# Two staging slots, a second DMA queue and ScalarE in the weight quantiser; preparation of the next tile placed ahead of the conv work in stage A

## The chip, the cores and the metric

The kernel runs as one program on the 8 cores of one Trainium2 chip. Each core computes one half of one batch entry's output; there are no messages between the cores. The metric is the device time in microseconds (us) of the slowest core. Engines of a core: TensorE (PE) for matmuls, VectorE (DVE), ScalarE (ACT), GpSimd (POOL), and SyncE (SP), which here only issues DMAs. POOL issues DMAs too; they stand on a queue of their own.

## The reference

One "macaron" layer: half an FFN, an attention-like recurrent block, and half the same FFN again. The layout is channels on partitions, positions along the free axis.

```
x = x + 0.5 * ffn(layernorm(x))
x = x + ssm_and_recurrence(layernorm(x))
x = x + 0.5 * ffn(layernorm(x))

ffn:  h = bit_linear(x, w1)            # 1024 -> 4096
      h = silu(depthwise_conv1d(h))    # 3 taps along the sequence
      return bit_linear(h, w2)         # 4096 -> 1024
bit_linear: act_quant:   s = 127 / max|x| per position; clip(round(x*s), -128, 127)/s
            weight_quant: s = 1 / mean|w|;              clip(round(w*s), -1, 1)/s
```

The rounding is done by adding a large constant and subtracting it again (columns `cmag` and `cnmag`).

## The kernel before

The program is written by hand, engine by engine, with counting semaphores. What is written down first for an engine runs first on it: an engine takes its own instructions in program order and waits where a wait is written. The helper `Sem.wait(engine)` without a value waits for everything that has been counted on that semaphore up to this point of the text, so a wait's place in the text also decides how much it waits for. Semaphores: `sv` DVE, `sa` ACT, `sp` PE, `sev` PSUM evictions, `sy` DMAs of SP, `sg` DMAs of POOL.

The stages in order of time:

- **Quantise w1** (`quant_weights`, 8 chunks of 128x4096 f32, 2 MB each). First loop: a chunk is loaded into the one staging slot (L350) and DVE sums its absolute values (L352). A few tiny operations turn the sums into the scale. Second loop: each chunk is loaded again (L381), DVE does three passes over it (L383 scale and add the magic constant, L386 subtract it and clip above, L390 clip below into `wq` as bf16), and SP stores the chunk to HBM (L392) for the second FFN. With one slot a load starts when DVE is done with the chunk before.
- **Stage A of FFN 1** (`ffn_stage_a`, 17 tiles of 256 positions with 2 of halo). A tile has 8 groups (`q` = 0 to 7). A group is 4 output banks of 8 matmuls each (L457, 32 in all), then ACT starts the conv from the banks (L466), DVE adds the two other taps (L474, L482; L482 also frees the banks), and ACT does Silu (L493). The matmuls of the next group wait for L482, as there are 4 banks. After Silu the text issues one step of the preparation of the next tile's input: `c_load` (group 0), `c_stats` (1), `c_ln` (2), `c_quant` (3), `c_smul` (4), `c_xq` (5). These use DVE, PE and ACT. After group 7 comes the quantisation of the tile's 4096 hidden channels (L297 to L529), which the change does not touch.
- **Quantise w2** (same function, 32 chunks of 128x1024 f32, 512 KB each), then **stage B of FFN 1** (matmuls with w2).
- **The middle block** (layer norms, scan, 18 sweeps of the recurrence, output projection), about 4500 to 7030 us.
- **Stage A of FFN 2** (9 tiles, the same function) and **stage B of FFN 2**. The quantised weights come back from HBM on POOL's queue.

Stage A therefore has 26 tiles, of which 24 prepare a next one (16 and 8).

Of the kernel before, what the change touches and what calls it, by code (L numbers as in the profile page):

```python
# [10 lines left out]
AF = mybir.ActivationFunctionType  # L11
ALU = mybir.AluOpType
AX = mybir.AxisListType
ds = bass.ds

P = 128
# [54 lines left out]
def build_nc(debug=False):  # L71
# [41 lines left out]
    with st:  # L113
        def sb(name, shape, dt=F32, stk=None):
            _nm[0] += 1
            return (stk or st).enter_context(nc.sbuf_tensor(f"{name}_{_nm[0]}", shape, dt))
# [8 lines left out]
        cmag = sb("cmag", [P, 1])  # L125
        cnmag = sb("cnmag", [P, 1])
# [4 lines left out]
        swcol = sb("swcol", [P, 1])  # L131
# [16 lines left out]
        cm = sb("cm", [P, 512])  # L148
# [17 lines left out]
        sy = Sem(st, nc, "sy")  # L166
        sg = Sem(st, nc, "sg")
        sv = Sem(st, nc, "sv")
        sa = Sem(st, nc, "sa")
# [4 lines left out]
        V, SC, T, G, SY = nc.vector, nc.scalar, nc.tensor, nc.gpsimd, nc.sync  # L174

        def tnop_inc(sem):
            T.drain()
            sem.inc(T.nop())

        def dma_fence():  # L180
            SY.wait_ge(sy.h, sy.n) if sy.n else None  # L181
            G.wait_ge(sg.h, sg.n) if sg.n else None

        def bar():
            dma_fence()
            nc.all_engine_barrier()
# [157 lines left out]

        def quant_weights(wsrc, nchunks, width, wq_t, wqhbm, rw_dst, wscb,
                          rw_scale=1.0 / 127.0):
            for c in range(nchunks):
                sv.wait(SY)
                dma_fence()
                sy.inc(SY.dma_start(wscb[:, 0:width], wsrc[c * P:(c + 1) * P, :]), 16)  # L350
                sy.wait(V)
                sv.inc(V.tensor_reduce(cm[:, c:c + 1], wscb[:, 0:width], AX.X,  # L352
                                       ALU.add, apply_absolute_value=True))
            V.drain()
            V.tensor_reduce(hmt[:, 0:1], cm[:, 0:nchunks], AX.X, ALU.add)
            sv.inc(V.drain())
            sv.wait(T)
            T.matmul(pst[0:1, 0:1], hmt[:, 0:1], onesf[:, 0:1], start=True, stop=True)
            tnop_inc(sp)
            sp.wait(V)  # L360
            V.tensor_scalar(r11[0:1, 0:1], pst[0:1, 0:1], 1.0 / (nchunks * P * width),
                            None, ALU.mult)
            V.drain()
            V.tensor_scalar(r11[0:1, 0:1], r11[0:1, 0:1], 1e-5, None, ALU.max)
            V.drain()
            V.reciprocal(r11[0:1, 1:2], r11[0:1, 0:1])
            V.drain()
            V.tensor_scalar(r11[0:1, 2:3], r11[0:1, 0:1], rw_scale, None, ALU.mult)
            sv.inc(V.drain())
            sv.wait(T)  # L370
            T.matmul(pst[0:P, 8:9], onesr[0:1, 0:P], r11[0:1, 1:2], start=True, stop=True)
            T.matmul(pst[0:P, 9:10], onesr[0:1, 0:P], r11[0:1, 2:3],
                     start=True, stop=True)
            tnop_inc(sp)
            sp.wait(V)
            V.tensor_copy(swcol[:, 0:1], pst[0:P, 8:9])
            V.tensor_copy(rw_dst[:, 0:1], pst[0:P, 9:10])
            sv.inc(V.drain())
            for c in range(nchunks):
                sv.wait(SY)  # L380
                sy.inc(SY.dma_start(wscb[:, 0:width], wsrc[c * P:(c + 1) * P, :]), 16)  # L381
                sy.wait(V)
                V.tensor_scalar(wscb[:, 0:width], wscb[:, 0:width], swcol[:, 0:1],  # L383
                                cmag[:, 0:1], ALU.mult, ALU.add)
                V.drain()
                V.tensor_scalar(wscb[:, 0:width], wscb[:, 0:width], cnmag[:, 0:1], 1.0,  # L386
                                ALU.add, ALU.min)
                V.drain()
                dst = wq_t[:, c * width:(c + 1) * width]
                sv.inc(V.tensor_scalar(dst, wscb[:, 0:width], -1.0, None, ALU.max))  # L390
                sv.wait(SY)
                sy.inc(SY.dma_start(wqhbm[c * P:(c + 1) * P, :], dst), 16)  # L392
            bar()

        def ffn_stage_a(wq, abuf, src_hbm, c0list, yq_hbm):
# [50 lines left out]
            for ti in range(nt):  # L446
                c0 = c0list[ti]
                xq_t = xqs[ti % 2]
                nxt = (prep_chunks(ti + 1, c0list[ti + 1]) if ti + 1 < nt
                       else [])  # L450
                sv.wait(T)
                for q in range(HC // 4):
                    for j in range(4):
                        mh = 4 * q + j
                        sev.wait(T, sev.n - 3 + j)
                        for kd in range(DC):
                            mm = T.matmul(pb[j][:, 0:tw],  # L457
                                          wq[:, kd * HD + mh * P:kd * HD + (mh + 1) * P],
                                          xq_t[:, kd * tw:(kd + 1) * tw],
                                          start=(kd == 0), stop=(kd == DC - 1))  # L460
                        sp.inc(mm)
                    sp.wait(SC)
                    SC.drain()
                    for j in range(4):
                        mh = 4 * q + j
                        a1 = SC.activation(tg[:, (mh % 8) * TOA:(mh % 8 + 1) * TOA],  # L466
                                           pb[j][:, 0:tw - 2], AF.Identity,
                                           bias=convbs[:, mh:mh + 1],
                                           scale=convws[:, 3 * mh:3 * mh + 1])
                    sa.inc(a1)  # L470
                    sa.wait(V)
                    for j in range(4):
                        mh = 4 * q + j
                        V.scalar_tensor_tensor(tg[:, (mh % 8) * TOA:(mh % 8 + 1) * TOA],  # L474
                                               pb[j][:, 1:tw - 1],
                                               convws[:, 3 * mh + 1:3 * mh + 2],
                                               tg[:, (mh % 8) * TOA:(mh % 8 + 1) * TOA],
                                               ALU.mult, ALU.add)
                    V.drain()
                    for j in range(4):  # L480
                        mh = 4 * q + j
                        ev = V.scalar_tensor_tensor(tg[:, (mh % 8) * TOA:(mh % 8 + 1) * TOA],  # L482
                                                    pb[j][:, 2:tw],
                                                    convws[:, 3 * mh + 2:3 * mh + 3],
                                                    tg[:, (mh % 8) * TOA:(mh % 8 + 1) * TOA],
                                                    ALU.mult, ALU.add)
                        sev.inc(ev)
                    sv.inc(V.engine_nop())  # L488
                    sv.wait(SC)
                    SC.drain()  # L490
                    for j in range(4):
                        mh = 4 * q + j
                        a2 = SC.activation(y2[:, mh * TOA:(mh + 1) * TOA],  # L493
                                           tg[:, (mh % 8) * TOA:(mh % 8 + 1) * TOA],
                                           AF.Silu)
                    sa.inc(a2)
                    if nxt:
                        nxt.pop(0)()
                sa.wait(V)
                quant_cols(y2, HC, TOA, None, 2,  # L500
                           acol_dst=a2col[:, c0 // 128:c0 // 128 + 2], halves=2)
# [83 lines left out]
        with ffn1:  # L585
# [16 lines left out]
            with sta:  # L602
                abuf = make_stage_a_bufs(sta)
                quant_weights(w1T, DC, HD, wq, wq1buf, rw1c, abuf[5], rw_scale=1.0)
                sv.wait(V)
                V.tensor_scalar(convws[:], convws[:], rw1c[:, 0:1], None, ALU.mult)
                sv.inc(V.drain())
                bar()
                ffn_stage_a(wq, abuf, xT, FF1_A, yqbuf)
            stb = ExitStack()  # L610
            with stb:
                xt = sb("xt", [P, DC * 512], F32, stb)
                yy = sb("yy", [P, DC * 512], F32, stb)
                yqb = sb("yqb", [P, HC * 512], BF16, stb)
                quant_weights(w2T, HC, D, wq, wq2buf, rw2h, yy, rw_scale=1.0)
                sv.wait(V)
                V.tensor_scalar(rw2h[:], rw2h[:], 0.5, None, ALU.mult)
                sv.inc(V.drain())
                bar()
                ffn_stage_b(wq, xt, yy, yqb, xT, FF1_B, yqbuf, x1buf)  # L620
# [455 lines left out]
```

How the kernel before makes its waits and increments, by code:

```python
    def inc(self, instr, by=1):  # L57
        instr.then_inc(self.h, by)
        self.n += by
        return instr
# [1 line left out]
    def wait(self, eng, val=None):  # L62
        v = self.n if val is None else val
        if v > 0:
            eng.wait_ge(self.h, v)
# [5 lines left out]
def build_nc(debug=False):  # L71
# [108 lines left out]
        def dma_fence():  # L180
            SY.wait_ge(sy.h, sy.n) if sy.n else None
            G.wait_ge(sg.h, sg.n) if sg.n else None
# [639 lines left out]
                        hw_marks = [sv.n]  # L822
                        ac_marks = []
                        g_all = 0
                        pend = []
                        for k in range(NSWEEP):
                            parR = (k % 2) * CPAR
                            parW = ((k + 1) % 2) * CPAR
                            for ti, (wi0, tn) in enumerate(UW_T):
                                for kap in range(KC):
                                    trip = ptrip[g_all % 2]
                                    T.wait_ge(sv.h, hw_marks[k])
                                    if g_all >= 2:
                                        sa.wait(T, ac_marks[g_all - 2])
                                    for gi, mpart in enumerate((kap, 4 + kap, 8 + kap)):
```

## Time and profile before

| what | value |
|---|---|
| median of 3 runs | 9121.12 us (9119.67 to 9121.30) |
| profiled execution, its own time | 9118.18 us |
| its span (core 3, the slowest) | 9116.6 us |
| spans of the 8 cores | 9068.4 to 9116.6 us |
| busy: PE, DVE, ACT, POOL | 3693.0, 3885.0, 1955.1, 32.4 us |
| mean granted TensorE clock, all cores | 0.687 to 0.691 |

No engine is busy for half of the span: 43% for DVE, 41% for PE. The time is in chains of waits, stage by stage, and a stage is read from its own rows. The granted clock is a share of full speed: 1.00 is 2.4 GHz, 0.50 is 1.2 GHz. A row of the windows view reads, from left to right: start and end in us, length, busy time (and number of instructions) of PE, of PE's weight loads, of DVE, ACT and POOL, then the granted clock, the mean busy share of the core's 16 DMA engines, and GB/s.

### The profile page before, as it was taken

What the parts mean: (1) busy time and instruction counts of PE and PEld (TensorE: products, weight loads), DVE (VectorE), ACT (ScalarE), POOL (GpSimd) and SP (SyncE); (2) the same over time, 40 slices, a digit from 0 to 9 for tenths busy, and PEclk for the clock granted to TensorE, in tenths of its full rate; (3) what the DMA queues carried; (4) which work ended last, traced back from release to release, by engine and by line L of the source; (5) the groups of instructions that cost most, each with busy time, mean ns of one, the idle gap of its engine ahead of it and who ended that gap; (6) DMA issues with size and microseconds to landing.
All of it is one profiled execution on the core that took longest, in us unless ns stands there. A gap on an engine that the chain in (4) does not pass through costs nothing. (4 is left out here: it accounts for less than half of the span.)

```text
span 9116.6 us, 55112 instructions; the slowest of 8 cores (9068.4 to 9116.6 us)
## 1 busy us (share of the span) xinstructions
PE 3693.0 (41%) x17682; PEld 1957.9 (21%) x17682; DVE 3885.0 (43%) x7213; ACT 1955.1 (21%) x3466; POOL 32.4 (0%) x59
## 2 busy tenths in 40 slices
PE   0222332332332310467522258888852233233257
PEld 0121221221221200223200023433320122122123
DVE  2454555545455432100165534444444454554400
ACT  0122222222222210000000005555530222222200
POOL 0000000000000000000000000000000000000000
PEclk9865665665666655778755579999975566566578
DMA  6200000000000013232211110000024000000042
GB/s 150 83 14 23 19 14 19 23 14 19 23 14 14 23 54 106 99 111 74 93 46 55 37 59 5 1 1 1 1 89 150 19 19 14 19 24 14 23 134 83
DMA packets 311196, 406.89 MB, mean 45 GB/s; under 512 B 20482, under 2 KB 224514, under 8 KB 305154
## 3 DMA queue, kind: packets, MB, share of 16 engines
q1 hardware_dynamic: 305186, 383.44, 13.1%
q0 software_dynamic: 5728, 19.93, 0.7%
q8 instruction: 148, 2.42, 0.1%
q14 instruction: 134, 1.10, 0.0%
HBM read 271.23 MB, written 135.26 MB: 45 GB/s over the span
## 5 line engine op out<-in xcount | busy, mean ns | idle before, releaser
L556 PE MATMUL pb<-yqb,wq 128*128 128x512 bf16 x3584 | 826.7, 396 | 344.1 <-DMA yqb<-yqbuf 222.9
L457 PE MATMUL pb<-xq,wq 128*128 128x258 bf16 x3584 | 623.7, 355 | 568.7 <-DVEq L526 375.0
L474 DVE SCALAR_TENSOR_TENSOR tg<-pb,convws,tg 128x256 f32<-128x256 f32 x832 | 345.1, 477 | 1167.5 <-ACT tg L466 1162.8
L457 PE MATMUL pb<-xqb,wq 128*128 128x258 bf16 x3072 | 531.5, 354 | 499.1 <-DVEq L526 375.3
L841 PE MATMUL pb<-cfc,WhS 128*128 128x512 bf16 (+1 forms) x2880 | 679.8, 365 | 0.0
L466 ACT ACTIVATE tg<-pb,convbs,convws 128x256 f32<-128x256 f32 x832 | 402.8, 566 | 964.7 <-PE pb L457 960.7
L457 PEld LDWEIGHTS pb<-xq,wq 128*128 128x128 bf16 x3584 | 446.5, 127 | 759.0 <-issue 610.7
L332 PE MATMUL pbc<-idsf,repb 128*128 128x128 f32 x316 | 89.4, 408 | 1136.1 <-DVE repb L327 1136.1
L562 DVE SCALAR_TENSOR_TENSOR yy<-pb,rw2h,xt 128x512 f32<-128x512 f32 x112 | 84.1, 751 | 1086.1 <-PE pb L556 1086.1
L556 PEld LDWEIGHTS pb<-yqb,wq 128*128 128x128 bf16 x3584 | 361.7, 101 | 805.9 <-issue 458.5
L457 PEld LDWEIGHTS pb<-xqb,wq 128*128 128x128 bf16 x3072 | 381.1, 126 | 662.4 <-issue 536.8
L522 DVE TENSOR_TENSOR yqa<-y,pbc 128x256 bf16<-128x256 f32 x832 | 280.0, 413 | 546.6 <-ACT y L517 546.6
L493 ACT ACTIVATE y<-tg 128x256 f32<-128x256 f32 x832 | 278.0, 405 | 666.8 <-DVEq L488 666.5
L250 PE MATMUL pst<-xbb,onesb 128*1 128x258 bf16 (+1 forms) x336 | 105.8, 496 | 719.0 <-DVE sqbb L247 719.0
L297 DVE TENSOR_REDUCE cm<-y 128x256 f32<-128x8192 f32 x26 | 359.6, 13832 | 43.3 <-ACT y L493 43.3
L302 PE MATMUL pst<-idsf,cm 128*128 128x128 f32 (+1 forms) x130 | 39.9, 432 | 805.6 <-DVE cm L297 805.6
L482 DVE SCALAR_TENSOR_TENSOR tg<-pb,convws,tg 128x256 f32<-128x256 f32 x832 | 345.0, 477 | 16.5 <-issue 0.9
L836 PE MATMUL pb<-Usb,idsb 128*128 128x512 bf16 (+1 forms) x720 | 262.8, 365 | 199.0 <-ACT tzb L855 111.7
L841 PEld LDWEIGHTS pb<-cfc,WhS 128*128 128x128 bf16 x2880 | 278.0, 103 | 282.6 <-issue 41.1
L841 PE MATMUL pst<-cfc,WhS 128*128 128x512 bf16 (+1 forms) x1440 | 329.1, 356 | 0.0
L515 ACT ACTIVATE y<-y,cmag 128x4096 f32<-128x4096 f32 x52 | 192.9, 3709 | 630.1 <-DVE repb L327 342.4
L861 DVE TENSOR_TENSOR dtb<-tfb,tzb 128x512 f32<-128x512 f32 (+1 forms) x180 | 110.2, 612 | 484.1 <-ACT tzb L855 484.1
(169 smaller groups left out, 4749.1 us busy)
## 6 DMA issues: line engine op xcount, KB each, us to landing
yqb<-yqbuf SPq DMA_DIRECT2D x9, 4096.0 KB
yqbuf<-yqa SPq DMA_DIRECT2D x34, 1024.0 KB
y<-w1T SPq DMA_DIRECT2D x16, 2048.0 KB
yy<-w2T SPq DMA_DIRECT2D x64, 512.0 KB
yqb<-yq2buf SPq DMA_DIRECT2D x5, 4096.0 KB
xt<-xT SPq DMA_DIRECT2D x9, 2048.0 KB
x1buf<-yy SPq DMA_DIRECT2D x9, 2048.0 KB
yq2buf<-yqa SPq DMA_DIRECT2D x18, 1024.0 KB
```

The source lines that it names most:

```text
L297: sv.inc(V.tensor_reduce(cm[:, 0:tw], ap3, AX.X, ALU.max, apply_absolute_value=True))
L457: mm = T.matmul(pb[j][:, 0:tw], wq[:, kd * HD + mh * P:kd * HD + (mh + 1) * P], xq_t[:, kd * tw:(kd + 1) * tw], start=(kd == 0), stop=(kd ...
L466: a1 = SC.activation(tg[:, (mh % 8) * TOA:(mh % 8 + 1) * TOA], pb[j][:, 0:tw - 2], AF.Identity, bias=convbs[:, mh:mh + 1], scale=convws[:, ...
L474: V.scalar_tensor_tensor(tg[:, (mh % 8) * TOA:(mh % 8 + 1) * TOA], pb[j][:, 1:tw - 1], convws[:, 3 * mh + 1:3 * mh + 2], tg[:, (mh % 8) * ...
L482: ev = V.scalar_tensor_tensor(tg[:, (mh % 8) * TOA:(mh % 8 + 1) * TOA], pb[j][:, 2:tw], convws[:, 3 * mh + 2:3 * mh + 3], tg[:, (mh % 8) * ...
L493: a2 = SC.activation(y2[:, mh * TOA:(mh + 1) * TOA], tg[:, (mh % 8) * TOA:(mh % 8 + 1) * TOA], AF.Silu)
L515: SC.activation(y2h, y2h, AF.Identity, bias=cmag[:, 0:1])
L522: V.tensor_tensor(yqa[:, c * TOA:(c + 1) * TOA], bass.AP(y2, (half * hh + c) * TOA, [[HC * TOA, P], [1, TOA]]), pbc2[:, 0:TOA], ALU.mult)
L556: mm = T.matmul(bank[:, 0:tw], wq[:, kh * D + md * P:kh * D + (md + 1) * P], yqb[:, kh * tw:(kh + 1) * tw], start=(kh == 0), stop=(kh == H ...
L836: T.matmul(trip[gi][:, 0:tn], idsb[:], Usb[:, mpart * WLEN + wi0: mpart * WLEN + wi0 + tn], start=True, stop=False)
L841: mm = T.matmul(trip[gi][:, 0:tn], WhS[:, kk * M3 + mpart * P:kk * M3 + (mpart + 1) * P], cfc[:, parR + kk * NCOL + wi0: parR + kk * NCOL ...
L861: V.tensor_tensor(da[:, 0:tn], tf_[:, 0:tn], tz_[:, 0:tn], ALU.mult)
```

## The change

There are two edits. `quant_weights` gets two staging slots (the buffers are wide enough already), even chunks go over SP's queue and odd ones over POOL's, each load waits only for the last reader of its own slot (`vmark`), and the two rounding passes move from DVE to ACT, so that one DVE pass is left, which clips on both sides. In stage A the call that issues the preparation step moves from the end of the group to a place right behind the group's matmuls, ahead of `sp.wait(SC)` and the conv work.

```diff
         def quant_weights(wsrc, nchunks, width, wq_t, wqhbm, rw_dst, wscb,
                           rw_scale=1.0 / 127.0):
+            def slot(c):
+                return wscb[:, (c % 2) * width:(c % 2) * width + width]
+            qs = [(sy, SY), (sg, G)]
+            dma_fence()
+            vmark = [sv.n, sv.n]
             for c in range(nchunks):
-                sv.wait(SY)
-                dma_fence()
-                sy.inc(SY.dma_start(wscb[:, 0:width], wsrc[c * P:(c + 1) * P, :]), 16)
-                sy.wait(V)
-                sv.inc(V.tensor_reduce(cm[:, c:c + 1], wscb[:, 0:width], AX.X,
+                sm, Q = qs[c % 2]
+                sv.wait(Q, vmark[c % 2])
+                sm.inc(Q.dma_start(slot(c), wsrc[c * P:(c + 1) * P, :]), 16)
+                sm.wait(V)
+                sv.inc(V.tensor_reduce(cm[:, c:c + 1], slot(c), AX.X,
                                        ALU.add, apply_absolute_value=True))
+                vmark[c % 2] = sv.n
...
+            vmark = [sv.n, sv.n]
             for c in range(nchunks):
-                sv.wait(SY)
-                sy.inc(SY.dma_start(wscb[:, 0:width], wsrc[c * P:(c + 1) * P, :]), 16)
-                sy.wait(V)
-                V.tensor_scalar(wscb[:, 0:width], wscb[:, 0:width], swcol[:, 0:1],
-                                cmag[:, 0:1], ALU.mult, ALU.add)
-                V.drain()
-                V.tensor_scalar(wscb[:, 0:width], wscb[:, 0:width], cnmag[:, 0:1], 1.0,
-                                ALU.add, ALU.min)
-                V.drain()
+                sm, Q = qs[c % 2]
+                sv.wait(Q, vmark[c % 2])
+                sm.inc(Q.dma_start(slot(c), wsrc[c * P:(c + 1) * P, :]), 16)
+                sm.wait(SC)
+                SC.drain()
+                SC.activation(slot(c), slot(c), AF.Identity,
+                              bias=cmag[:, 0:1], scale=swcol[:, 0:1])
+                SC.drain()
+                sa.inc(SC.activation(slot(c), slot(c), AF.Identity,
+                                     bias=cnmag[:, 0:1]))
+                sa.wait(V)
                 dst = wq_t[:, c * width:(c + 1) * width]
-                sv.inc(V.tensor_scalar(dst, wscb[:, 0:width], -1.0, None, ALU.max))
-                sv.wait(SY)
-                sy.inc(SY.dma_start(wqhbm[c * P:(c + 1) * P, :], dst), 16)
+                sv.inc(V.tensor_scalar(dst, slot(c), 1.0, -1.0, ALU.min, ALU.max))
+                vmark[c % 2] = sv.n
+                sv.wait(Q)
+                sm.inc(Q.dma_start(wqhbm[c * P:(c + 1) * P, :], dst), 16)
             bar()
...
                         sp.inc(mm)
+                    if nxt:
+                        nxt.pop(0)()
                     sp.wait(SC)
                     SC.drain()
...
                     sa.inc(a2)
-                    if nxt:
-                        nxt.pop(0)()
                 sa.wait(V)
```

How the instructions stand. DVE in stage A before, groups 0 to 2 of the first tile (L474 and L482 are the conv taps of a group, L246 to L274 are `c_stats`, ISA is the empty instruction that counts the group as done):

```order
L474 SCALAR_TENSOR_TENSOR tg<-pb,convws,tg 128x256 x4
L482 SCALAR_TENSOR_TENSOR tg<-pb,convws,tg 128x256 x4
L488 ISA
L474 SCALAR_TENSOR_TENSOR tg<-pb,convws,tg 128x256 x4
L482 SCALAR_TENSOR_TENSOR tg<-pb,convws,tg 128x256 x4
L488 ISA
L246 CAST xbb<-xta 128x2064
L247 TENSOR_TENSOR sqbb<-xta 128x2064
L261 TENSOR_SCALAR statr<-pst 1x258
```

The same place after (the conv taps are L486 and L494 there):

```order
L486 SCALAR_TENSOR_TENSOR tg<-pb,convws,tg 128x256 x4
L494 SCALAR_TENSOR_TENSOR tg<-pb,convws,tg 128x256 x4
L500 ISA
L246 CAST xbb<-xta 128x2064
L247 TENSOR_TENSOR sqbb<-xta 128x2064
L261 TENSOR_SCALAR statr<-pst 1x258
L262 TENSOR_SCALAR statr<-pst 1x258
L264 SCALAR_TENSOR_TENSOR statr<-pst,statr 1x258
L267 TENSOR_TENSOR statr<-statr 1x258
L272 RECIPROCAL statr<-statr 1x258
L274 TENSOR_TENSOR statr<-statr 1x258
L486 SCALAR_TENSOR_TENSOR tg<-pb,convws,tg 128x256 x4
```

The whole of `c_stats` now stands between the conv taps of group 0 and those of group 1, where before it stood behind those of group 1. The other steps move in the same way.

ACT in stage A before, at `c_smul` of the first tile (L338 and L342 are its two rounding passes, L466 the conv, L493 Silu; L318 and L320 belong to `c_quant`):

```order
L318 ACTIVATE stg<-tcol 128x3
L320 ACTIVATE stg<-stg 128x3
L466 ACTIVATE tg<-pb,convbs,convws 128x256 x4
L493 ACTIVATE y_45<-tg 128x256 x4
L338 ACTIVATE yya<-yya,cmag 128x2064
L342 ACTIVATE yya<-yya,cnmag 128x2064
```

The same engine and steps after (conv L478, Silu L505):

```order
L318 ACTIVATE stg<-tcol 128x3
L320 ACTIVATE stg<-stg 128x3
L478 ACTIVATE tg<-pb,convbs,convws 128x256 x4
L505 ACTIVATE y_45<-tg 128x256 x4
L338 ACTIVATE yya<-yya,cmag 128x2064
L342 ACTIVATE yya<-yya,cnmag 128x2064
```

The rows read alike, but the conv between them is that of group 4 before and that of group 3 after: the two rounding passes now precede the conv of their own group 4. PE's order does not change at all in stage A: a step's matmuls stood between two groups before, and stand there still.

POOL after, in the quantisation of w1 (L355 is the load of the first loop, L389 that of the second, L402 the store); before, POOL had no DMA until the middle block:

```order
L355 DMA y_45<-w1T 128x4096 x4
L389 DMA y_45<-w1T 128x4096
L402 DMA wq1buf<-wq 128x4096
L389 DMA y_45<-w1T 128x4096
L402 DMA wq1buf<-wq 128x4096
```

SP has the same five rows at that place, so a queue's next load stands behind the store of its last chunk.

## Rows read from the trace of the kernel before

**Rows 1.** Windows: the quantisation's four loops, then POOL's eight 1 MB loads in a burst.

```profile
72.97:178.87 105.90, 0.00 (x0) 0.00 (x0) 35.35 (x8) 0.00 (x0) 0.00 (x0) 1.00 0.43 159
182.15:327.00 144.85, 0.00 (x0) 0.00 (x0) 56.48 (x24) 0.00 (x0) 0.00 (x0) 1.00 0.47 174
3313.30:3488.20 174.90, 0.00 (x0) 0.00 (x0) 39.05 (x32) 0.00 (x0) 0.00 (x0) 0.50 0.30 96
3491.50:3718.50 227.00, 0.00 (x0) 0.00 (x0) 72.30 (x96) 0.00 (x0) 0.00 (x0) 0.50 0.34 111
7030.53:7056.40 25.87, 0.00 (x0) 0.00 (x0) 0.01 (x1) 0.00 (x0) 4.20 (x8) 0.50 0.80 324
```

**Rows 2.** Timeline, w1: one reduction, one clip; columns: start, duration, engine, line, operation.

```profile
96.36 4.42 DVE L352 TENSOR_REDUCE cm<-y 128x1 f32<-128x4096 f32 x1 [9.06 <-DMA y<-w1T]
...
195.29 2.29 DVE L390 TENSOR_SCALAR wq<-y 128x4096 bf16<-128x4096 f32 x1
```

**Rows 3.** Timeline, w2: one reduction and the clip of the second loop.

```profile
3486.89 1.22 DVE L352 TENSOR_REDUCE cm<-yy 128x1 f32<-128x1024 f32 x1 [4.70 <-DMA yy<-w2T]
...
3497.42 0.69 DVE L390 TENSOR_SCALAR wq<-yy 128x1024 bf16<-128x1024 f32 x1
```

**Rows 4.** Timeline, stage A: an ACT rounding pass over 4096 columns.

```profile
518.29 3.71 ACT L515 ACTIVATE y<-y,cmag 128x4096 f32<-128x4096 f32 x1 [13.15 <-DVE repb L327]
```

**Rows 5.** POOL's loads: eight of 1 MB (L959), 32 of 256 KB (L975).

```profile
DMA to landing us min/median/max: 5.1/12.6/19.4
...
DMA to landing us min/median/max: 4.0/9.3/12.6
```

**Rows 6.** Timeline, PE, stage A, second tile: matmuls of groups 1 to 6.

```profile
560.96 5.96 PE L457 MATMUL pb<-xqb,wq 128*128 128x258 bf16 x32 [4.55 <-DVE tg L482]
579.44 3.75 PE L457 MATMUL pb<-xqb,wq 128*128 128x258 bf16 x32
591.73 5.93 PE L457 MATMUL pb<-xqb,wq 128*128 128x258 bf16 x32 [0.31 <-issue]
608.53 6.06 PE L457 MATMUL pb<-xqb,wq 128*128 128x258 bf16 x32 [0.30 <-issue]
623.75 5.31 PE L457 MATMUL pb<-xqb,wq 128*128 128x258 bf16 x32 [0.30 <-issue]
639.96 5.72 PE L457 MATMUL pb<-xqb,wq 128*128 128x258 bf16 x32 [0.46 <-issue]
```

**Rows 7.** Timeline, same tile: conv taps and the preparation steps.

```profile
558.59 1.66 DVE L474 SCALAR_TENSOR_TENSOR tg<-pb,convws,tg 128x256 f32<-128x256 f32 x4 [8.67 <-ACT tg L466]
...
572.41 1.23 DVE L246 CAST xbb<-xta 128x2064 bf16<-128x2064 f32 x1
...
585.81 1.66 DVE L474 SCALAR_TENSOR_TENSOR tg<-pb,convws,tg 128x256 f32<-128x256 f32 x4 [0.20 <-issue]
...
589.37 1.20 PE L279 MATMUL pbc<-statr,onesr 1*128 1x258 f32 x2 [6.18 <-DVEq L488]
...
594.47 2.76 DVE L289 TENSOR_TENSOR yya<-yya,pbc 128x258 f32<-128x258 f32 x8
...
607.36 0.88 PE L302 MATMUL pst<-idsf,cm 128*128 128x128 f32 x3 [9.69 <-DVE cm L297]
...
609.73 0.20 ACT L318 ACTIVATE stg<-tcol 128x3 f32<-128x3 f32 x1 [5.01 <-DVE stg L315]
...
621.75 0.68 DVE L327 TENSOR_SCALAR repb<-ones,stg 128x128 f32<-128x128 f32 x3 [1.59 <-ACT y L493]
...
626.53 2.02 ACT L338 ACTIVATE yya<-yya,cmag 128x2064 f32<-128x2064 f32 x1 [4.88 <-DVEq L427]
...
630.77 1.94 ACT L466 ACTIVATE tg<-pb,convbs,convws 128x256 f32<-128x256 f32 x4
```

**Rows 8.** Windows: the matmuls of `c_stats`, then those of group 2 (same columns).

```profile
576.01:579.44 3.43, 3.43 (x17) 1.87 (x17) 0.00 (x0) 0.00 (x0) 0.00 (x0) 0.52 0.00 0
579.44:583.19 3.75, 3.75 (x33) 3.03 (x32) 1.58 (x4) 1.72 (x2) 0.00 (x0) 1.00 0.00 0
```

## The prediction

> **What bounds the kernel now.** I read the busy shares first: no engine reaches half of the span, so each stage has to be read by itself. The windows over the four loops of the weight quantiser [rows 1] come next: 105.90, 144.85, 174.90 and 227.00 us, 652.65 us together, with PE and ACT at nothing, DVE busy for 203 us of it and the DMA share at 0.30 to 0.47. The timelines say why [rows 2, 3]: a reduction of w1 waits 9.06 us for its load and then takes 4.42 us, one of w2 waits 4.70 and takes 1.22. Load and work take turns, since there is one slot. Last I read one stage A tile on all engines [rows 6, 7]. From group to group PE starts 18.48, 12.29, 16.80, 15.22 and 16.21 us apart (groups 1 to 6, 79.00 us). The loop is matmuls, ACT conv, DVE taps, next matmuls; a restart comes 2.37 us after the first tap begins (558.59 to 560.96). The preparation step lies behind the taps, and most of its DVE and ACT work runs beside the next group's matmuls.
>
> **The quantiser, first loops.** Two loads are now in flight. What they can reach together: POOL's eight loads moved 8 MB at 324 GB/s [rows 1], so 2.1 MB need 6.4 us at best. For w1 I follow the two slots: both first loads share the rate and land after 14.5 us, the reductions end at 18.9 and 23.4, then each slot repeats load (some 2 us until data moves, alone at first, shared later) and 4.42 us of reduction, 14.7 us per pair. That gives 67.5 us for 8 chunks in place of 105.90: 38 saved. Ends: 58 us, if the rate is always full (48 saved), and 78, if a pair overlaps badly (28 saved).
> For w2 a slot's round is load, reduction, issue. 256 KB on POOL's queue land after 4.0 us at the least and 1 MB after 5.1 [rows 5]; SP's 512 KB take 4.7 [rows 3]. I take 5.3 with both in flight, plus 1.22 and 0.2: 6.7 us per pair, 3.35 per chunk, 110 us with the tail in place of 174.90: 65 saved. Ends: 2.7 per chunk (86 saved) and 4.3 (37 saved).
>
> **The quantiser, second loops.** ACT takes 3.71 us for 4096 columns [rows 4] and 2.02 for 2064 [rows 7], so 0.83 ns per column and 1.16 us for 1024. Two passes with their drains are 7.6 us for w1 and 2.55 for w2. DVE keeps one pass, 2.29 and 0.69 [rows 2, 3]; the clip on both sides has one source and one target as before, so I take the same duration. For w1 a slot's round is 3 MB of traffic (store, then load; some 10.3 us with the other slot's) and 10.2 us of ACT, DVE and issue: 20.5 per pair, near to 3.15 MB / 324 GB/s = 9.7 us per chunk. With 14.5 us until the first pair is there and a last store it is 102 us in place of 144.85: 43 saved (ends 56 and 25). For w2: load 5.0, ACT 2.55, DVE 0.9 with its semaphores, two issues at 0.53 on POOL's queue (4.20 us for 8 [rows 1]) come to 9.1 per pair, 4.55 per chunk, 150 us in place of 227.00: 77 saved (ends: 4.05 per chunk, 92 saved; 6.0, 30 saved). ACT was idle here, and what it gets hides behind loads.
> Sum of the quantiser: 38 + 65 + 43 + 77 = 223 us saved, between 120 and 282.
>
> Two-port passes of DVE are where a page speaks against this edit. The trace shows L390 over 4096 f32 columns in 2.29 us [rows 2] where the reduction takes 4.42, so this pass runs at twice the rate. The Trainium skill, "SBUF — State Buffer", "SBUF: two separate sides", says that a DVE pass in such a mode locks GpSimd out of a shared port pair, and that a DMA issued from GpSimd then waits for its descriptors. By that rule POOL's DMAs of the second loops could each wait out one clip: at most 8 of 2.29 and 32 of 0.69 us. No DVE pass and POOL DMA lie side by side in the trace of before, so it cannot tell.
>
> **Stage A, per tile with a next one.** The step now stands ahead of its own group's conv, and its PE part ahead of `sp.wait(SC)`, so the conv waits for the step's matmuls, and the taps for its DVE work. What was hidden beside the next matmuls comes onto the loop; what a step no longer has to wait for goes. From rows 6 and 7, matmuls first and restart last:
> - `c_load`: SP issues earlier, behind the fence on the last store. Nobody waited for this load in steady state; nothing.
> - `c_stats`: 5.96 + 0.05 + 13.40 (L246 at 572.41 to the next possible tap at 585.81; the ACT conv of 1.94 fits beside the reciprocal) + 2.37 = 21.78, was 18.48: +3.30.
> - `c_ln`: group 2's matmuls. They take 3.75 us now, at a granted clock of 1.00, coming straight behind 3.43 us of statistics matmuls at 0.52 [rows 8]. After the change 8 us of idle time lie between, and all other groups, which follow idle time, take 5.31 to 6.06. So 5.9 + 7.86 (L279 at 589.37 to the end of L289 at 597.23) + 0.10 + 2.37 = 16.23, was 12.29: +3.94, of which 2.15 is the clock.
> - `c_quant`: its long reduction can now run beside group 3's matmuls. 5.93 + 0.1 + 2.37 (607.36 to 609.73) + 0.35 + 2.04 for the conv + 2.37 = 13.16, was 16.80: -3.64.
> - `c_smul`: 6.06 + 0.1 + 4.78 (621.75 to 626.53) + 4.24 (two rounding passes on ACT, to 630.77) + 2.04 + 2.37 = 19.59, was 15.22: +4.37. Before, only the end of the ACT passes stuck out; now conv and taps queue behind all of it.
> - `c_xq`: 5.8 + 0.1 + 4.78 (the same chain of column broadcast and 8 multiplications) + 2.37 = 13.05, was 16.21: -3.16. The conv lies beside it.
> Sum: +4.81 us per tile, 24 tiles: +115 us. Ends: if group 2 keeps its fast matmuls and the statistics and layer-norm matmuls run at full clock too, the tile costs about nothing (0 us). If all five groups run at 1.2 GHz throughout (32 x 258 columns, 6.88 us each, 4.75 more per tile), it is +230.
>
> **Sum.** Against the profiled execution of 9118.18 us (span 9116.6): 9118 - 223 + 115 = 9010. The median of the runs is 3 us above that execution, which makes 9013.
>
> **Rivals.**
> 1. *POOL's queue is the slow half of each pair.* DVE and ACT take the chunks in order, so the slower queue sets the round. For: its 32 loads of 256 KB have a median of 9.3 us to landing [rows 5]. Against: these stood in a burst, and the least was 4.0. At 9.3 for every load of w2 the rounds are 10.7 and 13.6 us, 5.3 and 6.8 per chunk, and some 5 us of w2's gain remain; w1 keeps 81. 9118 - 86 + 115 = 9147, slower. It decides from about 8 us to landing, where the saving falls to what stage A loses.
> 2. *Stage A costs nothing*, because the clock stays up and the moved matmuls get faster. For: groups come closer to steps in two places, and one group already runs at 1.00 [rows 8]. Against: every group that follows idle time is slow [rows 6]. 9118 - 223 = 8895.
> 3. *Two loads in flight bring little*, because the cores that share memory all do this at once. For: a single load already moves at a good part of the rate. Against: 324 GB/s in the burst with 159 here [rows 1]. With the low end of every loop: 9118 - 120 + 115 = 9113, no change.
> 4. *Stage A at its dear end*, all groups at 1.2 GHz: 9118 - 223 + 230 = 9125, no change, slightly slower at worst.
> 5. *DVE's clip holds POOL's DMAs up.* In terms of this kernel: half of the second loops' chunks start their load up to one clip later, 4 x 2.29 + 16 x 0.69 = 20 us. 9033. This is the page's rule above with a chance of its own.
>
> **How the numbers follow.** Forecast 0.62, rival 5 0.08, rival 2 0.14, rival 3 0.05, rival 4 0.05, rival 1 0.06. A difference within 0.2% (18 us) can't be told from none. Forecast and rivals 2 and 5 are faster: 0.84. Rival 3 and part of rival 4 are the same: 0.08. Rival 1 and the rest are slower: 0.08. The range for 8 in 10 takes in the forecast's own uncertainty (some 40 us in each half of the sum), rival 5 and part of rival 2: 8925 to 9090.
>
> **What would show it.** In the windows of the quantiser: about 68, 102, 110 and 150 us. In stage A: groups 1 to 6 spread over about 83.8 us in place of 79.0, group 2's matmuls near 5.9 us, the first tap of group 4 behind L342, and L297's short form beside matmuls. ACT's busy time up by 8 x 7.4 + 32 x 2.3 = 133 us and DVE's down by about 88. I would be wrong on the mechanism if stage A tiles got shorter, or if the w2 loops kept more than 5.5 us per chunk; a wait of ACT or DVE for POOL's load alone would then be rival 1.

## The result and the profile after

| | before | after |
|---|---|---|
| median of 6 runs, us | 9121.21 (9117.94 to 9165.99) | 8991.00 (8981.07 to 9001.34) |
| ratio, time after over time before | | 0.9849, 95% interval 0.9829 to 0.9869 |
| profiled execution, its own time | 9118.18 | 8996.92 |
| span of the slowest core | 9116.6 (core 3) | 8995.4 (core 0) |
| busy: PE, DVE, ACT, POOL | 3693.0, 3885.0, 1955.1, 32.4 | 3690.6, 3799.0, 2088.8, 64.3 |

The kernel is 130 us (1.5%) faster. One more execution of it is on record, at 9043.77 us, which the median does not count. ACT's busy time rose by 133.7 us and DVE's fell by 86.0, against 133 and 88 in the prediction, so the arithmetic moved as written.

The slowest core is another one than before, and cores differ by up to 55 us in these two profiled executions, so stages are compared on one core. Core 3 went from 9116.6 to 8978.6, 138.0 less. First its four quantiser loops after; start:end and length, then busy PE, weight loads, DVE, ACT, POOL, granted clock, DMA share and GB/s; they answer to [rows 1]:

```profile
72.60:143.80 71.20, 1.17 (x6) 1.03 (x6) 36.12 (x15) 0.00 (x0) 2.27 (x4) 1.00 0.70 236
144.00:248.70 104.70, 0.00 (x0) 0.00 (x0) 18.39 (x9) 61.34 (x17) 4.22 (x8) 1.00 0.67 240
3287.70:3390.20 102.50, 1.17 (x6) 1.03 (x6) 39.92 (x39) 0.00 (x0) 8.44 (x16) 0.50 0.48 164
3390.40:3551.30 160.90, 0.00 (x0) 0.00 (x0) 22.22 (x32) 76.38 (x64) 17.10 (x32) 0.50 0.48 157
```

Read the GB/s column: 159, 174, 96 and 111 before, 236, 240, 164 and 157 now, for the same bytes. With the few microseconds between the loops counted in (each stage lasts from its first load to the first load or operation of the next one), core 3 has:

| core 3, us | before | after | difference | predicted |
|---|---|---|---|---|
| w1, first loop | 109.2 | 71.4 | -37.8 | -38 |
| w1, second loop | 145.0 | 104.7 | -40.3 | -43 |
| w2, first loop | 178.2 | 102.7 | -75.5 | -65 |
| w2, second loop | 227.0 | 160.9 | -66.1 | -77 |
| stage A of FFN 1 (16 tiles with a next) | 2985.4 | 3038.2 | +52.8 | +77 |
| stage A of FFN 2 (8 tiles with a next) | 1591.9 | 1619.4 | +27.5 | +38 |
| all else (by difference) | | | +1.4 | 0 |
| span | 9116.6 | 8978.6 | -138.0 | -108 |

Now w2's loops close up, on core 0. First loop: the reductions and POOL's loads, to be read against [rows 3], where each reduction waited 4.70 us.

```profile
3292.10 1.22 DVE L357 TENSOR_REDUCE cm<-yy 128x1 f32<-128x1024 f32 x1 [1.00 <-DMA yy<-w2T]
3293.89 0.53 POOL L355 DMA_DIRECT2D yy<-w2T  x1 [6.76 <-DVE cm L357]
3295.27 1.22 DVE L357 TENSOR_REDUCE cm<-yy 128x1 f32<-128x1024 f32 x1 [1.94 <-DMA yy<-w2T]
3298.08 1.22 DVE L357 TENSOR_REDUCE cm<-yy 128x1 f32<-128x1024 f32 x1 [1.59 <-DMA yy<-w2T]
3299.85 0.53 POOL L355 DMA_DIRECT2D yy<-w2T  x1 [5.44 <-DVE cm L357]
```

The wait is down to 1 to 2 us. POOL issues 0.57 us after the reduction that frees its slot ends (3292.10 + 1.22 to 3293.89; 0.55 us the next time), and one round of its slot is 5.96 us (3293.89 to 3299.85), for two chunks. I had 6.7, with a landing time of 5.3 us and 0.2 us for the issue; over the loads of L355, both queues and both weights, the landing took 4.1 in the median:

```profile
L355 POOL DMA_DIRECT2D yy<-w2T x16: 527/527/530, 3286.6 to 3377.6; - x16
...
DMA to landing us min/median/max: 4.0/4.1/16.1
```

Second loop: ACT's two passes, DVE's clip, POOL's store and load.

```profile
3401.19 1.24 ACT L392 ACTIVATE yy<-yy,cmag,swcol 128x1024 f32<-128x1024 f32 x1 [0.99 <-DMA yy<-w2T]
...
3402.50 1.15 ACT L395 ACTIVATE yy<-yy,cnmag 128x1024 f32<-128x1024 f32 x1
3403.75 0.69 DVE L399 TENSOR_SCALAR wq<-yy 128x1024 bf16<-128x1024 f32 x1 [2.76 <-ACT yy L395]
3405.00 0.55 POOL L402 DMA_DIRECT2D wq2buf<-wq  x1 [7.47 <-DVE wq L399]
...
3405.54 0.53 POOL L389 DMA_DIRECT2D yy<-w2T  x1
...
3413.58 0.55 POOL L402 DMA_DIRECT2D wq2buf<-wq  x1 [7.52 <-DVE wq L399]
```

From store to store POOL's slot takes 8.58 us here; over all 16 stores it is 9.5 on the mean. I had 9.1, and 4.4 us for both ends of the loop (150 less 16 rounds). On this core the first POOL store is issued 10.2 us into the loop, and the last, at 3539.35, stands 6.7 us before the barrier is passed (3546.05): 10.2 + 15 x 9.53 + 6.7 = 159.8 us. So the rounds are some 7 us longer than I had them and the ends some 3.

Stage A, second tile on core 0: matmuls of groups 1 to 6, which answer to [rows 6].

```profile
482.46 5.99 PE L467 MATMUL pb<-xqb,wq 128*128 128x258 bf16 x32 [4.54 <-DVE tg L494]
504.43 5.28 PE L467 MATMUL pb<-xqb,wq 128*128 128x258 bf16 x32 [8.67 <-DVE tg L494]
519.11 6.42 PE L467 MATMUL pb<-xqb,wq 128*128 128x258 bf16 x32 [8.35 <-DVE tg L494]
532.13 5.08 PE L467 MATMUL pb<-xqb,wq 128*128 128x258 bf16 x32 [6.27 <-DVE tg L494]
550.46 6.12 PE L467 MATMUL pb<-xqb,wq 128*128 128x258 bf16 x32 [11.72 <-DVE tg L494]
563.96 6.19 PE L467 MATMUL pb<-xqb,wq 128*128 128x258 bf16 x32 [5.86 <-DVE tg L494]
```

Each group now waits for the taps (L494), where before five of these six stood behind a preparation step's own matmuls. What lies in between, to be read against [rows 7]:

```profile
502.06 1.66 DVE L486 SCALAR_TENSOR_TENSOR tg<-pb,convws,tg 128x256 f32<-128x256 f32 x4 [0.20 <-issue]
...
509.63 0.70 PE L279 MATMUL pbc<-statr,onesr 1*128 1x258 f32 x2
...
513.81 2.76 DVE L289 TENSOR_TENSOR yya<-yya,pbc 128x258 f32<-128x258 f32 x8
...
520.27 3.90 DVE L297 TENSOR_REDUCE cm<-yya 128x258 f32<-128x2064 f32 x1
...
541.82 2.02 ACT L338 ACTIVATE yya<-yya,cmag 128x2064 f32<-128x2064 f32 x1 [7.17 <-DVEq L437]
...
546.06 1.93 ACT L478 ACTIVATE tg<-pb,convbs,convws 128x256 f32<-128x256 f32 x4
548.09 1.66 DVE L486 SCALAR_TENSOR_TENSOR tg<-pb,convws,tg 128x256 f32<-128x256 f32 x4 [6.39 <-ACT tg L478]
```

L297 runs beside group 3's matmuls (519.11 to 525.53), and the conv of group 4 stands behind ACT's two rounding passes, with PE idle for 11.72 us. Both are as forecast. L279 is the surprise: 0.70 us in place of 1.20. The clocks of group 2's matmuls, of L279 and L280 behind them, and of group 4's matmuls (same columns as above, the clock is the third number from the end):

```profile
504.43:509.71 5.28, 5.28 (x33) 3.89 (x33) 1.03 (x3) 2.62 (x5) 0.00 (x0) 0.69 0.00 0
509.63:510.76 1.13, 1.13 (x5) 0.66 (x4) 0.00 (x0) 0.00 (x0) 0.00 (x0) 1.00 0.00 0
...
532.13:537.21 5.08, 5.08 (x32) 3.72 (x32) 1.03 (x3) 1.33 (x4) 0.00 (x0) 0.72 0.00 0
```

Before, L279 stood at 0.50 and group 4's matmuls at 0.60.

| step, us from group to group | before | predicted | after |
|---|---|---|---|
| `c_stats` (1 to 2) | 18.48 | 21.78 | 21.97 |
| `c_ln` (2 to 3) | 12.29 | 16.23 | 14.68 |
| `c_quant` (3 to 4) | 16.80 | 13.16 | 13.02 |
| `c_smul` (4 to 5) | 15.22 | 19.59 | 18.33 |
| `c_xq` (5 to 6) | 16.21 | 13.05 | 13.50 |
| sum | 79.00 | 83.81 | 81.50 |

### The profile page after: what moved, and what is told of

The parts are those of the page before. It is cut to its first block and busy times, and to the rows that moved or that the text cites. A ratio compares the mean times of both kernels' runs of the same rounds, so it can differ in the third digit from the quotient of the medians.

```text
span 8995.4 us, 55001 instructions; the slowest of 8 cores (8940.2 to 8995.4 us)
## 1 busy us (share of the span) xinstructions
PE 3690.6 (41%) x17501; PEld 1971.0 (22%) x17682; DVE 3799.0 (42%) x7133; ACT 2088.8 (23%) x3546; POOL 64.3 (1%) x119
## 5 line engine op out<-in xcount | busy, mean ns | idle before, releaser
L467 PE MATMUL pb<-xq,wq 128*128 128x258 bf16 x3584 | 659.7, 370 | 1041.5 <-DVE tg L494 659.2
L467 PE MATMUL pb<-xqb,wq 128*128 128x258 bf16 x3072 | 568.2, 371 | 972.3 <-DVE tg L494 596.5
L467 PEld LDWEIGHTS pb<-xq,wq 128*128 128x128 bf16 x3584 | 465.2, 132 | 1240.7 <-issue 1074.8
L486 DVE SCALAR_TENSOR_TENSOR tg<-pb,convws,tg 128x256 f32<-128x256 f32 x832 | 345.0, 477 | 900.5 <-ACT tg L478 886.5
L467 PEld LDWEIGHTS pb<-xqb,wq 128*128 128x128 bf16 x3072 | 400.2, 133 | 1144.8 <-issue 1001.3
L478 ACT ACTIVATE tg<-pb,convbs,convws 128x256 f32<-128x256 f32 x832 | 401.3, 563 | 747.5 <-PE pb L467 546.1
L505 ACT ACTIVATE y<-tg 128x256 f32<-128x256 f32 x832 | 277.5, 404 | 777.6 <-DVEq L500 777.3
L297 DVE TENSOR_REDUCE cm<-y 128x256 f32<-128x8192 f32 x26 | 359.6, 13831 | 43.7 <-ACT y L505 43.7
L332 PE MATMUL pbc<-idsf,repb 128*128 128x128 f32 x316 | 72.5, 341 | 691.9 <-DVE repb L327 691.9
L494 DVE SCALAR_TENSOR_TENSOR tg<-pb,convws,tg 128x256 f32<-128x256 f32 x832 | 345.0, 477 | 16.4 <-issue 0.9
L515 DVE TENSOR_TENSOR y<-y,pbc 128x256 f32<-128x256 f32 x832 | 277.8, 409 | 26.3 <-PEq L178 26.3
L846 PE MATMUL pb<-Usb,idsb 128*128 128x512 bf16 (+1 forms) x666 | 238.0, 357 | 123.2 <-ACT tzb L865 104.5
```

What stands on the lines that cost most here:

```text
L297: sv.inc(V.tensor_reduce(cm[:, 0:tw], ap3, AX.X, ALU.max, apply_absolute_value=True))
L467: mm = T.matmul(pb[j][:, 0:tw], wq[:, kd * HD + mh * P:kd * HD + (mh + 1) * P], xq_t[:, kd * tw:(kd + 1) * tw], start=(kd == 0), stop=(kd ...
L505: a2 = SC.activation(y2[:, mh * TOA:(mh + 1) * TOA], tg[:, (mh % 8) * TOA:(mh % 8 + 1) * TOA], AF.Silu)
L515: V.tensor_tensor(y2[:, c * TOA:(c + 1) * TOA], y2[:, c * TOA:(c + 1) * TOA], pbc[:, 0:TOA], ALU.mult)
L846: T.matmul(trip[gi][:, 0:tn], idsb[:], Usb[:, mpart * WLEN + wi0: mpart * WLEN + wi0 + tn], start=True, stop=False)
```

## The experiments

Edits are given against the changed kernel, shortened, with `...` where lines are left out. "Steps late" means that the preparation call stands at the end of the group, as before. The kernel before, run on the same chips, had medians of 9110 to 9130; each ratio is against its own of them, so where two experiments were compared with different ones, ratios are the safer comparison. Each trace shown is that of the run's slowest core unless another is named.

### One part of the change alone

`quant_only`, steps late:

```diff
-                    if nxt:
-                        nxt.pop(0)()
                     sp.wait(SC)
...
                     sa.inc(a2)
+                    if nxt:
+                        nxt.pop(0)()
```

> The new weight quantiser with the preparation steps at their old place. Theory (the two edits are independent and add up): all of the saving and none of the loss in stage A, so 8991 - 80 = about 8910 us; stage A tiles back at 174.0 us. Rival (the stages interact, by memory traffic or by cores drifting apart, and the saving of the quantiser is partly given back later): above 8950.

Measured: 8896.54 us (8893.69 to 8925.43), ratio 0.9762 (0.9733 to 0.9792).

`stage_only`, the same move of the call made in the kernel before, with its quantiser:

> The old quantiser with the preparation steps ahead of the conv work. Theory: 24 tiles at +3.3 us, 9121 + 80 = about 9201 us. Rival (the step's new place is itself a gain that the trace comparison hides, for instance by other cores): 9121 or less.

Measured: 9210.36 us (9196.24 to 9229.38), ratio 1.0103 (1.0075 to 1.0131). By ratio the quantiser saves 217 us of 9121 and the move costs 94 (68 to 119). Together that is -123, and the whole change has -138 (-119 to -156). The edits add up within these intervals, and one of the two is a loss: the quantiser alone is 94 us faster than the whole change by the medians, 79 by the ratios. The traces measure the loss more closely. Both stages A together, from their first load to the first load of the stage behind them, take on the mean of the eight cores 4576.2 us before, 4577.0 in `quant_only`, 4659.4 after and 4659.6 in `stage_only`: the move costs 83 us with either quantiser, 3.5 per tile.

### What in the quantiser saves

`one_queue`, steps late, both slots on SP's queue:

```diff
-            qs = [(sy, SY), (sg, G)]
+            qs = [(sy, SY), (sq, SY)]      # sq: a new semaphore
...
+            sq.wait(SY)
             bar()
```

> The quantiser-only kernel (8897 us) with both slots on SP's queue, each with a semaphore of its own. In the first loops only loads stand on the queue; in the second loops the next load stands behind the store of the chunk before, and so behind its arithmetic. Theory (it is the load that runs beside the arithmetic that saves, and POOL's queue is only the way to it): first loops unchanged, 71 and 100 us; second loops as good as serial with the longer arithmetic of ACT and DVE, about 160 and 270 us; together 165 us more, about 9060. Rival (two slots are enough, the queue does not matter): 8900.

Measured: 9049.90 us, ratio 0.9935 (0.9919 to 0.9952). Its four loops on core 2:

```profile
69.40:138.40 69.00, 1.17 (x6) 1.04 (x6) 36.33 (x15) 0.00 (x0) 0.00 (x0) 1.00 0.74 243
138.40:308.00 169.60, 0.00 (x0) 0.00 (x0) 18.36 (x9) 61.34 (x17) 0.00 (x0) 1.00 0.40 148
3290.70:3383.80 93.10, 1.17 (x6) 1.04 (x6) 40.03 (x39) 0.00 (x0) 0.00 (x0) 0.50 0.56 180
3383.80:3638.60 254.80, 0.00 (x0) 0.00 (x0) 22.21 (x33) 76.37 (x64) 0.00 (x0) 0.50 0.31 99
```

The first loops keep their whole gain on one queue; w2's is even shorter than with POOL (93.1 us, 100.9 in `quant_only` on core 0). That fits SP's sooner issue (see the last section), but was not tested by itself. The second loops are worse than those of the kernel before [rows 1], 169.60 and 254.80 against 144.85 and 227.00: the load waits behind the store, the store behind the arithmetic, and the arithmetic is longer when it passes from ACT to DVE. So what saves is a load issued ahead of the arithmetic of the chunk before. In the second loops the other queue is the only way to that as the text is ordered.

`dve_round`, steps late, the three passes of a chunk on DVE again:

```diff
-                sm.wait(SC)
...                                     # both SC.activation and their drains go
-                sa.wait(V)
+                sm.wait(V)
+                V.tensor_scalar(slot(c), slot(c), swcol[:, 0:1], cmag[:, 0:1], ALU.mult, ALU.add)
+                V.drain()
+                V.tensor_scalar(slot(c), slot(c), cnmag[:, 0:1], 1.0, ALU.add, ALU.min)
+                V.drain()
```

> The quantiser-only kernel with the three rounding passes back on DVE, two slots and two queues kept. Theory (the move to ACT brings nothing, since a chunk's arithmetic of 7.2 us of w1 and 2.5 of w2 on DVE is shorter than on ACT and DVE together, and loads bound the loops): 8897 or up to 20 us less. Rival 1 (the split over ACT and DVE is part of the saving): 20 to 60 us more. Rival 2 (DVE's two-port passes hold the DMAs of POOL's queue up, now with three of them per chunk): POOL's loads land later than the 5.3 us of median in the changed kernel and the second loops get longer.

Measured: 8868.98 us (8864.72 to 8886.17), ratio 0.9737 (0.9721 to 0.9754), 28 us under `quant_only` by the medians and 23 by the ratios, whose intervals overlap. Its loops took 73.5, 96.8, 97.9 and 143.3 us (core 6) where `quant_only` has 69.6, 106.3, 100.9 and 155.0 (core 0). Core by core the picture is the same: on cores 0, 3, 4 and 7 the second loop is 11 to 14 us shorter for w1 and 8 to 20 for w2, while the first loops, which the edit does not touch, differ by at most 3.2 us. So the move to ACT was no gain but a loss of some 20 to 30 us: a slot's round takes in the arithmetic, and that is longer on ACT and DVE together. On the rival with POOL's DMAs, POOL's issues of L389 in `dve_round` and then in `quant_only`:

```profile
L389 POOL DMA_DIRECT2D yy<-w2T x16: 527/621/840, 3323.3 to 3451.6; - x16
...
DMA to landing us min/median/max: 3.9/4.8/15.1
```

```profile
L389 POOL DMA_DIRECT2D yy<-w2T x16: 527/527/530, 3333.0 to 3472.3; - x16
...
DMA to landing us min/median/max: 4.3/4.7/14.6
```

With three two-port passes of DVE per chunk an issue of w2 takes 621 ns in the median and up to 840 on this core, with one it never takes over 530; the landing stays the same (4.8 and 4.7). The passes of w1 are longer, and there the hold is longer too. On core 0 of `dve_round`:

```profile
185.93 2.41 DVE L391 TENSOR_SCALAR y<-y,swcol,cmag 128x4096 f32<-128x4096 f32 x1 [1.03 <-DMA y<-w1T]
185.98 2.48 POOL L389 DMA_DIRECT2D y<-w1T  x1
```

POOL's issue begins inside a DVE pass and ends 0.12 us after it (188.46 and 188.34), 1.95 us late. So do all the others: every issue of POOL over 0.6 us in the second loops of `dve_round`, on all eight cores, ends 0.11 to 0.13 us after the end of a DVE pass. Of w1's 64 loads and stores on POOL's queue 6 were held, on four cores. This is the lock of the Trainium skill, "SBUF — State Buffer", "SBUF: two separate sides"; the trace agrees, with these 0.12 us. The second loops are the shorter ones all the same. In the changed kernel, with one pass per chunk, no load of L389 took over 530 ns and no store over 552 on any core, so there it costs nothing.

`four_slots`, steps late, four slots for w2:

```diff
+            ns = 4 if nchunks > 8 else 2
-            qs = [(sy, SY), (sg, G)]
+            qs = [(sy, SY), (sg, G), (sq, SY), (sr, G)]   # load(c): wait for the slot's mark, issue
...
+            for c in range(ns):                            # ahead of each of the two loops
+                load(c)
...
+                if c + ns < nchunks:                       # at the end of a chunk
+                    load(c + ns)
...
+            sq.wait(SY)
+            sr.wait(G)
```

> The quantiser-only kernel with four staging slots for w2 (two per queue, a semaphore for each, the load of a slot issued right behind the store of its last chunk); w1 as it was. Theory (the w2 loops are bound by the round of a slot, latency and not bytes): first loop from 3.1 to about 1.9 us per chunk, 60 us; second from 5.0 to about 2.9, bound by ACT, 100 us; 100 us less in all, about 8797. Rival (the DMAs are bound by bytes or by the traffic of the neighbour core): less than 30 us less.

Measured: 8797.22 us (8791.47 to 8824.60), ratio 0.9653 (0.9636 to 0.9669). Its two loops of w2, on core 1:

```profile
3226.00:3293.40 67.40, 1.17 (x6) 1.03 (x6) 38.94 (x39) 0.00 (x0) 8.44 (x16) 0.50 0.73 249
3293.40:3395.20 101.80, 0.00 (x0) 0.00 (x0) 22.27 (x33) 76.40 (x64) 17.11 (x32) 0.50 0.71 247
```

67 and 102 us at 249 and 247 GB/s: with two slots these loops were bound by a slot's round, not by bytes. (60 and 100 us were expected, and 100.9 and 155.0 are those of `quant_only`, so the loops saved 87 us, on these two cores, where 100 were expected. That the whole came out at the expected 8797 us is in part luck.)

### Single steps of stage A

All have the new quantiser, and one or two steps early, the rest late; `if nxt` gets a condition at both places:

```diff
-                    if nxt:
+                    if nxt and q == 1:      # stats_early; q in (0, 1): load_stats_early
                         nxt.pop(0)()        # q == 4: smul_early; q == 5: xq_early
```

> The new quantiser; only c_stats (group 1) is issued ahead of the conv work. Theory (group 2's matmuls were fast only because the statistics matmuls stood straight before them): group 1 to 2 takes 3.3 to 3.5 us more, and group 2's matmuls go from 3.75 to 5.3 us or more and push the next group by 1.5, about 5 us per tile, 120 us over the quantiser-only kernel, about 9030. Rival (the clock follows the work of the whole tile, not its order): group 2's matmuls stay at 3.75, only 3.3 per tile, 80 us.

Measured: 9069.77 us (9065.25 to 9119.77), ratio 0.9945 (0.9925 to 0.9966), 40 us more than expected. Groups 1, 2 and 3 (core 6):

```profile
671.11 5.92 PE L467 MATMUL pb<-xq,wq 128*128 128x258 bf16 x32 [4.54 <-DVE tg L494]
694.79 6.01 PE L467 MATMUL pb<-xq,wq 128*128 128x258 bf16 x32 [8.68 <-DVE tg L494]
708.98 5.76 PE L467 MATMUL pb<-xq,wq 128*128 128x258 bf16 x32 [0.39 <-issue]
```

Group 2's matmuls went from 3.75 to 6.01 us, so their speed did hang on the statistics matmuls right before them. But 1 to 2 took 23.68 in place of some 21.9, and the cause is in its trace:

```profile
673.75 0.37 SPq L417 DMA_DIRECT2D xta<-xT  x1
678.97 1.24 DVE L246 CAST xbb<-xta 128x2064 bf16<-128x2064 f32 x1 [6.83 <-DMA xta<-xT]
```

The late load is issued 2.64 us after group 1's matmuls begin, and the early statistics wait for it. Both stages A take 4744.1 us on the mean of the cores, 167 more than in `quant_only` or 7.0 per tile.

> The new quantiser; c_load (group 0) and c_stats (group 1) are issued ahead of the conv work, the rest behind it. With c_stats alone ahead, group 1 to 2 took 23.7 us, 5.3 more than before, while in the changed kernel it took 22.0. Theory (there c_stats waited for a load that was issued late): group 1 to 2 takes 21.9 us, group 2's matmuls 5.9, the tile about 5.2 us more than in the quantiser-only kernel, 8897 + 125 = about 9020 us. Rival (the load plays no part): 23.7 us again and about 9070.

Measured: 8973.09 us (8963.82 to 9041.31), ratio 0.9873 (0.9832 to 0.9913). The same three groups (core 2):

```profile
655.11 5.89 PE L467 MATMUL pb<-xq,wq 128*128 128x258 bf16 x32 [4.54 <-DVE tg L494]
676.98 5.22 PE L467 MATMUL pb<-xq,wq 128*128 128x258 bf16 x32 [8.67 <-DVE tg L494]
690.37 5.35 PE L467 MATMUL pb<-xq,wq 128*128 128x258 bf16 x32 [0.39 <-issue]
```

1 to 2 is 21.87, as expected: the load's place is worth 1.8 us there. Both stages A take 4660.5 us, 83.6 less than in `stats_early`, so over the whole tile it is worth 3.5 us once the statistics are early. The time is 47 us below what I expected by the medians and 24 by the ratios, since group 2's matmuls took 5.22 and not 5.9, and later groups were faster as well. In `stats_early` the same matmuls, behind the same statistics matmuls and the same 8.7 us of idle time, took 6.01; what differs in the rows is the idle time ahead of the statistics matmuls, 5.55 us there and 3.71 here. And 4660.5 is what the changed kernel takes (4659.4): load and statistics early cost as much as the whole move, and moving the four other steps as well changes nothing in sum.

> The quantiser-only kernel (8897 us) with c_smul alone ahead of the conv work. Theory (conv and taps queue behind its 8 multiplications and ACT's two rounding passes): group 4 to 5 takes 18.3 to 19.6 us in place of 15.2, 24 tiles at +3.1 to 4.4: 8971 to 9002 us. Rival (a clock that rises with the denser matmuls, as it did with c_xq, pays it back): within 20 us of 8897.

Measured: 8936.78 us (8928.09 to 8944.74), ratio 0.9799 (0.9782 to 0.9815). 40 us over `quant_only` (34 by the ratios), between both theories. Both stages A take 4604.2 us on the mean, 27 more than in `quant_only`, and cores differ here: 4595.6 to 4616.8. Groups 4 to 7 of a tile on core 0:

```profile
2102.98 6.07 PE L467 MATMUL pb<-xq,wq 128*128 128x258 bf16 x32 [0.30 <-issue]
2122.30 4.99 PE L467 MATMUL pb<-xq,wq 128*128 128x258 bf16 x32 [11.72 <-DVE tg L494]
2136.44 4.75 PE L467 MATMUL pb<-xq,wq 128*128 128x258 bf16 x32 [0.30 <-issue]
2145.73 5.21 PE L467 MATMUL pb<-xq,wq 128*128 128x258 bf16 x32 [4.53 <-DVE tg L494]
```

4 to 5 is 19.32, as the step's sum had it. What I left out is the next group: with the step late, ACT's rounding passes push group 5's conv back by 1.6 us, and that is gone, so 5 to 6 falls from 16.1 to 14.1 and 6 to 7 from 10.3 to 9.3, with faster matmuls.

> The new quantiser; of the preparation steps only c_xq (group 5) is issued ahead of the conv work, the others stand behind it as before. Theory (a step gains at the early place when what it needs is done during the matmuls, since it no longer waits for Silu): groups 5 to 6 take about 14.3 us in place of 16.2, 1.9 us per tile, 24 tiles: 45 us under the quantiser-only kernel, about 8865. Rival (any step at the early place is a loss, because the conv waits behind it): above the quantiser-only kernel.

Measured: 8809.19 us (8804.71 to 8813.99), ratio 0.9654 (0.9630 to 0.9679), 87 us under `quant_only`; 45 were expected. Both stages A take 4495.6 us, 81 less. Groups 5 to 7 (core 4):

```profile
711.36 5.31 PE L467 MATMUL pb<-xq,wq 128*128 128x258 bf16 x32 [0.30 <-issue]
725.27 5.19 PE L467 MATMUL pb<-xq,wq 128*128 128x258 bf16 x32 [5.52 <-DVE tg L494]
734.99 5.38 PE L467 MATMUL pb<-xq,wq 128*128 128x258 bf16 x32 [4.54 <-DVE tg L494]
```

5 to 6 is 13.91 (16.08 in `quant_only`), 6 to 7 is 9.72 (10.31), and groups 0 and 1 start 10.32 apart in place of 10.68. The whole tile is 170.2 in place of 173.7. Some 2.2 of the 3.5 us are the step, the rest are shorter matmuls elsewhere; the mean granted clock went from 0.690 to 0.699.

### The version that beats both

`four_slots_xq` has four slots for w2 and only `c_xq` early; `four_slots_xq_dve` also rounds w1 on DVE.

> Four staging slots for w2 and only c_xq ahead of the conv work. Theory (the quantiser and stage A share nothing, so the two gains add up): 8797 - 87 = about 8710 us, 4.5% under the kernel before. Rival (part of the gain of c_xq was chance of the chip's clock): about 8750.

Measured: 8725.21 us (8719.98 to 8729.69), ratio 0.9572 (0.9556 to 0.9588).

> The same with the rounding of w1 (two slots) on DVE and that of w2 (four slots) on ACT. Theory (w1's second loop has a slot's round as its bound, and 7.2 us on DVE are shorter than 10.2 on ACT and DVE): 8 to 10 us under the kernel beside it. Rival (bytes bound that loop): the same time.

Measured: 8718.58 us (8714.93 to 8728.76), ratio 0.9565 (0.9549 to 0.9581). The two gains add up within 15 us by the medians and 25 by the ratios, and both stages A of `four_slots_xq` take 4495.7 us, as in `xq_early`. The 7 us of DVE's rounding are within the intervals, so that question is open for w1. The best version is 4.3% faster than the kernel before and 3% faster than the changed one.

## Why the prediction was right

- **The sum.** 9013 forecast, 8991 measured, inside 8925 to 9090. Both terms have the forecast sign and are separate, as `quant_only` and `stage_only` show. The quantiser saved 219.7 us on core 3 (223 forecast). Stage A cost 80.3 there and 83 on the mean of all cores, where 115 were forecast: the sign is right, the size is over a third too large.
- **Quantiser.** The rounds of a slot were the right model. That the sum came within 4 us is luck in part, as the two w2 terms were off by 11 us each in opposite directions: loads land after 4.1 us and not 5.3 in the first loop (POOL's start behind the reduction takes 0.56 us where I had 0.2), and the second loop has a slower mean round and ends that are some 3 us longer than I had them. That ACT's work "hides behind loads" was wrong for the second loops: it is part of a slot's round, and `dve_round` is faster. The sum of the prediction had it in the round, its closing sentence did not.
- **`c_load` at nothing.** Right for the sum, as it moved together with the statistics; alone it is worth 3.5 us per tile, since the early statistics need it early (`stats_early` against `load_stats_early`).
- **`c_stats`, `c_quant`, `c_xq`.** Within 0.5 us.
- **`c_ln` and `c_smul`** were mis-sized, by 1.55 and 1.26 us, and both by PE's clock: I took 5.9 us for group 2's matmuls and full length for L279, L280 and L332, from groups that follow long idle time. After the change a step's matmuls come straight behind the group's or 1 us later; group 2's took 5.28 (clock 0.69), L279 0.70 for 1.20 (1.00 for 0.50), group 4's matmuls 5.08 for 6.06 (0.72 for 0.60). The clocks are read off; what raises them was not tested by itself. Against that, groups 6 and 7 became slower (6.19 and 5.96 us, 5.72 and 5.37 before), which is how 2.5 us between groups 1 and 6 become 3.3 per tile (80.3 over 24).
- **Rivals.** POOL's queue as the slow half: no, 4.1 us to landing. (Its second round should read 13.4 us and not 13.6, by the prediction's own terms; it changes nothing.) A byte limit: no, `four_slots` reached 249 GB/s in w2's loops and `dve_round` 260 in w1's second. DVE holding POOL up: not in the changed kernel, where no issue was held; with three passes per chunk it is there, up to 1.95 us at a time. Stage A for nothing: no, 83 us by the traces and 94 (68 to 119) by `stage_only`, but with part of its reason, the moved matmuls being faster. Its dear end: no.

## What to carry to other kernels

Take a change of two edits apart before judging it: here a gain of some 220 us covered a loss of some 83. When a step is moved ahead of a wait, write down for every engine what now stands in front of the next critical instruction, and do the sum for the step's neighbours too: a step is cheap at the early place only if it is short and its inputs are done. For staging loops compute a slot's round (issue, landing, arithmetic, store), divide by the slots, and see which engine or queue becomes the limit before that: for `four_slots` it gave 60 and 100 us for loops that took 67 and 102. Arithmetic in a slot's round is not hidden, even on an idle engine.

## What was not expected of the hardware

- Matmul groups of the same 32 instructions took 3.75 to 6.42 us, at granted clocks of 1.00 and 0.56, and small moves shifted the whole tile: `xq_early`, `load_stats_early` and `smul_early` ran at a mean granted clock near 0.70, `quant_only` at 0.69. In `xq_early` this gave up to 1.3 us per tile. Which order of work raises it was not settled; it was read off, not tested by itself.
- POOL starts a DMA 0.55 to 0.57 us after the DVE instruction that it waited for has ended; SP does so 0.08 us after (3392.67 + 0.69 to 3393.44 in the second w2 loop).
- Stage B of FFN 1, which no edit touches, took 769 us on core 0 in the profiled execution before and 791 after, on core 4 771 and 790, on core 3 793 and 794. Core 0 was 22.5 us quicker than core 3 before and is 16.8 slower after; 21 of these 39 us are stage B's. The cause was not looked for.
